# Adjacency blocks as sums of three bf16 products, with the one-hot operands of two blocks interleaved

## The reference, cut to what matters

```python
def _spmm(row, col, val, x):
    return jax.ops.segment_sum(val[:, None] * x[col], row, num_segments=N)
h = _spmm(edge_row, edge_col, edge_val, inputs_emb)
...
    z = _spmm(edge_row, edge_col, edge_val, outputs)      # layers 0 and 1
    AxW = jax.nn.softmax(z @ W.T + b, axis=1)
...
xn = _layernorm(x, axis=-1)
x = x + _L0_gnn_ref(xn, ..., edge_weight, src, dst) + _L0_mix_ref(xn[None], ...)[0]
x = x + _L0_ffn_ref(_layernorm(x, axis=-1)[None], ...)[0]
```

## Time and profile before

| | us |
|---|---|
| median of 3 runs | 1162.5 (1161.41 to 1164.13) |
| span of the profiled execution | 1161.9 |
| TensorE busy | 1097.3 (94%) |
| TensorE weight loads busy | 701.6 |
| VectorE busy | 737.1 (63%) |
| ScalarE busy | 314.2 (27%) |
| GpSimd busy | 168.1 (14%) |
| block matmuls (L1527), busy | 171.3 |
| products with the adjacency (L1542), busy | 291.8 |

### The profile page before, as it was taken

How to read it: one execution, slowest core, us unless ns; L and a number is a source line. 1 busy time by engine, 2 the same in 40 slices (tenths; PEclk the granted TensorE clock), 3 DMA queues, 4 the chain that set the end, 5 groups by cost and what they waited for, 6 DMA issues and landing times.

```text
span 1161.9 us, 14112 instructions
## 1 busy us (share of the span) xinstructions
PE 1097.3 (94%) x4837; PEld 701.6 (60%) x4837; DVE 737.1 (63%) x1681; ACT 314.2 (27%) x1038; POOL 168.1 (14%) x206
## 2 busy tenths in 40 slices
PE   5879999999999999999998999999998799999995
PEld 3446666666666666667793444644447666666664
DVE  8989989998786877777760111116788435554444
ACT  4667767421211222122210111101112211122220
POOL 1112223301010100000000000000234511111111
PEclk9899989999999999999998999999999799999998
DMA  5110111123323223343318998997995584555520
GB/s 168 18 45 13 46 47 46 46 91 121 133 96 133 114 112 121 126 154 136 131 57 323 325 354 292 343 343 275 308 320 213 155 217 117 118 141 136 141 63 7
DMA packets 78871, 178.52 MB, mean 154 GB/s; under 512 B 33567, under 2 KB 62011, under 8 KB 66639
## 3 DMA queue, kind: packets, MB, share of 16 engines
q1 hardware_dynamic: 67550, 126.16, 34.1%
q10 hardware_dynamic: 7120, 43.34, 9.2%
q0 software_dynamic: 4128, 8.08, 2.0%
HBM read 116.23 MB, written 63.77 MB: 155 GB/s over the span
## 4 chain that ended last, share of the span: by engine, by line
PE 80%; DVE 9%; SPq 3%; issue 3%; ACT 2%; DMA 1%; POOLq 0%; POOL 0%; ACTq 0%; DVEq 0%
PE ps L1542 21%; PE ps L1691 20%; PE ps L1527 11%; PE ps L1791 10%; PE ps L1779 9%; PE ps L1566 2%; SPq L465 2%; PE ps L1509 2%; PE ps L1442 1%; PE ps L1495 1%; DVE W L1022 1%; SPq L463 1%; DVE XT L1357 1%; ACT W L746 1%; PE ps L1516 1%
## 5 line engine op out<-in xcount | busy, mean ns | idle before, releaser
L1542 PE MATMUL ps<-RING,XX 128*128 128x512 f32 (+2 forms) x700 | 291.8, 542 | 1.0 <-DVE W L1082 1.0
L1691 PE MATMUL ps<-RING,RY 128*128 128x512 f32 (+4 forms) x750 | 273.7, 523 | 5.8 <-issue 5.8
L1691 PEld LDWEIGHTS ps<-RING,RY 128*128 128x128 f32 x750 | 136.8, 196 | 126.4 <-issue 119.0
L1527 PEld LDWEIGHTS ps<-RING 128*128 128x128 f32 x1250 | 164.5, 193 | 40.8 <-issue 34.1
L774 ACT COPY RING<-ps 128x512 f32<-128x512 f32 (+3 forms) x163 | 91.2, 560 | 312.2 <-PE ps L1527 298.2
L1527 PE MATMUL ps<-RING 128*128 128x128 f32 (+1 forms) x1250 | 171.3, 277 | 0.1
L1542 PEld LDWEIGHTS ps<-RING,XX 128*128 128x128 f32 x700 | 118.5, 191 | 68.8 <-issue 60.7
L1073 DVE TENSOR_TENSOR RING<-iota_n,RY 128x512 f32<-128x512 f32 (+1 forms) x138 | 91.2, 661 | 34.5 <-PE ps L1527 31.8
L1074 DVE TENSOR_TENSOR RING<-iota_n,RY 128x512 f32<-128x512 f32 (+1 forms) x138 | 100.5, 728 | 0.0
L1076 DVE TENSOR_TENSOR RING<-RING,RY 128x512 f32<-128x512 f32 (+1 forms) x138 | 91.1, 660 | 0.0
L900 ACT ACTIVATE RY<-ps,b1T 128x489 f32<-128x489 f32 x64 | 42.9, 670 | 172.2 <-PE ps L1779 172.2
(11 more groups left out here) (258 smaller groups left out, 1295.3 us busy)
## 6 DMA issues: line engine op xcount, KB each, us to landing
RING<-adj_dram SPq DMA_DIRECT2D x60, 1280.0 KB, 6.9
adj_dram<-RING ACTq DMA_DIRECT2D x30, 1280.0 KB, 4.5
rbuf_dram<-W SPq DMA_DIRECT2D x8, 516.0 KB, 5.4
RING<-rbuf_dram SPq DMA_DIRECT2D x8, 516.0 KB, 4.0
xbuf_dram<-W SPq DMA_DIRECT2D x8, 512.0 KB, 3.3
XT<-in_L_ffn_w SPq DMA_DIRECT2D x16, 256.0 KB, 5.1
XT<-in_L_ffn_w SPq DMA_DIRECT2D x4, 1024.0 KB, 8.4
RING<-in_L_ffn_w SPq DMA_DIRECT2D x16, 256.0 KB, 4.9
```

Source lines behind the costliest of these rows:

```text
L1527: last = nc.tensor.matmul(o[:, c:c + w], h[:, 0, i, :], h[:, 1, i, 0:w], start=True, stop=(j != s))
L1542: last = nc.tensor.matmul(ps[:, ACC + dd, 0:w], XN[:, j, dd * H:(dd + 1) * H], at[:, i * w:(i + 1) * w], start=(j == 0), stop=True, skip_g ...
L1691: last = nc.tensor.matmul(o, (Y if l == 0 else S0)[:, j, :], RING[:, slot_of[g % 5], i * across + first:i * across + first + w], start=(j ...
```

## The change

From unit 25 on a block is no longer one f32 product but the sum of three bf16 products: one one-hot matrix, all in bf16, times the other one-hot matrix multiplied by each of the three bf16 pieces of the value. The value now goes into the second operand. The operands of two neighbouring blocks are interleaved, so that the last dimension of every operand of VectorE is a pair of bf16 numbers (`pair_b`), and TensorE reads every second element. `recs` becomes a bf16 table; the f32 sum of the pieces, which only the lead needs, goes into `lead_w`. So that pairs begin at even groups, the extra group of the diagonal blocks is moved from place 25 to place 23 (`SPARE`), and tiles 23 and 24 to places 24 and 25 (`place_in`). Strip 5 works on two pairs, the second with the extra group as its unused half. A diagonal block takes three more products from `own_src` and `own_val`, which VectorE makes in four small operations. In the lead the matmuls stay in f32; ScalarE scales the extra group too, in four units.

```diff
+SPARE = 23
...
+def place_in(t):
+    return t if t < SPARE else t + 1
...
-        recs = RY[:, 0:5 * NG].rearrange("p (f n) -> p f n", f=5)
+        recs = RY[:, 0:1625].bitcast(BF16).rearrange("p (f n) -> p f n", f=5)
+        lead_w = RY[:, 1626:2276]
...
-        hot = [ring[:, 7680 + 1280 * i:8960 + 1280 * i].rearrange("p (a g n) -> p a g n", a=2, n=P) for i in range(4)]
+        hot_w = [ring[:, 7680 + 1280 * i:8960 + 1280 * i] for i in range(4)]
+        hot = [h.rearrange("p (a g n) -> p a g n", a=2, n=P) for h in hot_w]
+        hot_b = [h.bitcast(BF16) for h in hot_w]
+        pair_b = [h[:, 0:2048].rearrange("p (a c k i) -> p a c k i", a=4, c=2, i=2) for h in hot_b]
+        own_src = [h[:, 2048:2176] for h in hot_b]
+        own_val = [h[:, 2176:2560].rearrange("p (a k) -> p a k", a=3) for h in hot_b]
...
+        iota_p = sb("iota_p", [P, 2 * P], BF16)
...
-            gp.iota(ints[:, 416:416 + SW], pattern=[[1, NR], [0, WC]], base=0, channel_multiplier=0).then_inc(s_const, 1)
+            gp.iota(ints[:, 416:416 + SPARE * WC], pattern=[[1, SPARE], [0, WC]], base=0, channel_multiplier=0).then_inc(s_const, 1)
+            gp.iota(ints[:, 416 + SPARE * WC:416 + (SPARE + 1) * WC], pattern=[[0, WC]], base=EXTRA, channel_multiplier=0).then_inc(s_const, 1)
+            gp.iota(ints[:, 416 + (SPARE + 1) * WC:416 + SW], pattern=[[1, NT - SPARE], [0, WC]], base=SPARE, channel_multiplier=0).then_inc(s_const, 1)
...
+                    whole = lead_w[:, j * NR:(j + 1) * NR]
                     gp.wait_ge(s_recrd, j + 1)
-                    gp.tensor_tensor(w1, w1, w2, ALU.add).then_inc(s_wpart, 1)
+                    gp.tensor_tensor(whole, w1, w2, ALU.add).then_inc(s_wpart, 1)
                     gp.wait_ge(s_wpart, j + 1)
-                    gp.tensor_tensor(w1, w1, w3, ALU.add).then_inc(s_wsum, 1)
+                    gp.tensor_tensor(whole, whole, w3, ALU.add).then_inc(s_wsum, 1)
...
-                for i, (j, s) in enumerate(UNITS[u]):
-                    last = nc.scalar.activation(hot[u % 4][:, 0, i, :], hot[u % 4][:, 0, i, :], ACT.Copy, scale=recs[:, 2, j * NR + s:j * NR + s + 1])
+                blocks = list(enumerate(UNITS[u])) + [(4, (j, SPARE)) for j, s in UNITS[u] if j == s]
+                for i, (j, s) in blocks:
+                    last = nc.scalar.activation(hot[u % 4][:, 0, i, :], hot[u % 4][:, 0, i, :], ACT.Copy, scale=lead_w[:, j * NR + s:j * NR + s + 1])
...
+            v.tensor_scalar(iota_p[:, :], ints[:, 160:160 + 2 * P], -1.0 - OWN, None, ALU.add)
...
-                h = hot[u % 4]
+                own = [t for t, g in b if t == g]
                 if u < LEAD:
                     dve.wait_ge(s_wsum, u + 1)
-                own = [t for t, g in b if t == g]
-                if own:
-                    i = own[0] * NR + EXTRA
-                    v.tensor_scalar(h[:, 0, 4, :], iota_n[:, :], recs[:, 0, i:i + 1], recs[:, 2, i:i + 1], ALU.is_equal, ALU.mult)
-                    v.tensor_scalar(h[:, 1, 4, :], iota_n[:, :], recs[:, 1, i:i + 1], None, ALU.is_equal)
-                if u < LEAD:
+                    h = hot[u % 4]
+                    for t in own:
+                        i = t * NR + SPARE
+                        for a in range(2):
+                            v.tensor_scalar(h[:, a, 4, :], iota_n[:, :], recs[:, a, i:i + 1], None, ALU.is_equal)
                     v.tensor_tensor(h[:, :, 0:n, :], iota_n[:, :].unsqueeze(1).unsqueeze(1).to_broadcast([P, 2, n, P]),
                                     recs[:, 0:2, j * NR + s:j * NR + s + n].unsqueeze(3).to_broadcast([P, 2, n, P]), ALU.is_equal).then_inc(s_hot, 1)
                     return
-                if u < NT * (NS - 1):
-                    grid = lambda f: recs[:, f, j * NR + s:j * NR + s + n].unsqueeze(2).to_broadcast([P, n, P])
-                    every = iota_n[:, :].unsqueeze(1).to_broadcast([P, n, P])
-                    block = lambda a: h[:, a, 0:n, :]
-                else:
-                    grid = lambda f: recs[:, f, :].rearrange("p (t g) -> p t g", g=NR)[:, j:j + n // 2, s:s + 2].unsqueeze(3).to_broadcast([P, n // 2, 2, P])
-                    every = iota_n[:, :].unsqueeze(1).unsqueeze(1).to_broadcast([P, n // 2, 2, P])
-                    block = lambda a: h[:, a, 0:n, :].rearrange("p (t g) n -> p t g n", g=2)
-                v.tensor_tensor(block(0), every, grid(0), ALU.is_equal).then_inc(s_eq, 1)
-                v.tensor_tensor(block(1), every, grid(1), ALU.is_equal)
+                if u == LEAD:
+                    dve.wait_ge(s_recrd, NT)
+                heads = [j * NR + s, j * NR + s + 2] if u < NT * (NS - 1) else [t * NR + place_in(s) for t in range(j, j + n // 2)]
+                views = [(pair_b[u % 4][:, :, c], recs[:, :, first:first + 2], iota_p[:, :].rearrange("p (k i) -> p k i", i=2)) for c, first in enumerate(heads)]
+                for h, fields, every in views:
+                    wide = lambda x, m: x.unsqueeze(2).to_broadcast([P, m, P, x.shape[-1]])
+                    last = v.tensor_tensor(h[:, 0:4:3], every.unsqueeze(1).to_broadcast([P, 2, P, fields.shape[-1]]), wide(fields[:, 0:2], 2), ALU.is_equal)
+                last.then_inc(s_eq, 1)
+                for t in own:
+                    i = t * NR + SPARE
+                    v.tensor_scalar(own_src[u % 4], iota_n[:, :], recs[:, 0, i:i + 1], None, ALU.is_equal)
+                    for f in range(3):
+                        v.tensor_scalar(own_val[u % 4][:, f, :], iota_n[:, :], recs[:, 1, i:i + 1], recs[:, 2 + f, i:i + 1], ALU.is_equal, ALU.mult)
                 dve.wait_ge(s_eq, u + 1 - LEAD)
-                v.tensor_tensor(block(0), block(0), grid(2), ALU.mult).then_inc(s_hot, 1)
+                for h, fields, every in views:
+                    last = v.tensor_tensor(h[:, 1:4], h[:, 3:4].to_broadcast([P, 3, P, fields.shape[-1]]), wide(fields[:, 2:5], 3), ALU.mult)
+                last.then_inc(s_hot, 1)
...
+                piece = lambda a, i, w: pair_b[u % 4][:, a, i // 2, 0:w, i % 2]
                 ge(pe, s_bev, u - 1)
                 pe.wait_ge(s_wgt if u < LEAD else s_hot, u + 1)
                 for i, (j, s) in enumerate(UNITS[u]):
-                    c = width(g for _, g in UNITS[u][:i])
+                    c = width(t for _, t in UNITS[u][:i])
                     w = width([s])
-                    last = nc.tensor.matmul(o[:, c:c + w], h[:, 0, i, :], h[:, 1, i, 0:w], start=True, stop=(j != s))
+                    if u < LEAD:
+                        last = nc.tensor.matmul(o[:, c:c + w], h[:, 0, i, :], h[:, 1, i, 0:w], start=True, stop=(j != s))
+                        if j == s:
+                            last = nc.tensor.matmul(o[:, c:c + w], h[:, 0, 4, :], h[:, 1, 4, 0:w], start=False, stop=True)
+                        continue
+                    for f in range(3):
+                        last = nc.tensor.matmul(o[:, c:c + w], piece(0, i, P), piece(1 + f, i, w), start=(f == 0), stop=(f == 2 and j != s))
                     if j == s:
-                        last = nc.tensor.matmul(o[:, c:c + w], h[:, 0, 4, :], h[:, 1, 4, 0:w], start=False, stop=True)
+                        for f in range(3):
+                            last = nc.tensor.matmul(o[:, c:c + w], own_src[u % 4], own_val[u % 4][:, f, 0:w], start=False, stop=(f == 2))
```

More of the change, by code:

```diff
@@ L619, in _ @@
                              base=0, pattern=[[1, P]], channel_multiplier=-1).then_inc(s_const, 1)
-            gp.wait_ge(s_const, 9)
+            gp.wait_ge(s_const, 11)
             gp.memset(blk, 0.0).then_inc(s_blk, 1)
@@ L705, in _ @@
             act.dma_start(wv_n, half("L0_mix_wv")).then_inc(s_kvw, 16)
-            act.wait_ge(s_const, 9)
+            act.wait_ge(s_const, 11)
             nc.scalar.copy(before[:, :], before_f).then_inc(s_constb, 1)
@@ L941, in _ @@
             v.tensor_scalar(tile_no[:, :], thr[:, :], 1.0 / P, None, ALU.mult)
-            dve.wait_ge(s_const, 6)
+            dve.wait_ge(s_const, 8)
             v.tensor_copy(iota_n[:, :], ints[:, 32:32 + P])
             v.tensor_copy(iota_k[:, :], ints[:, 160:160 + 2 * P])
+            v.tensor_scalar(iota_p[:, :], ints[:, 160:160 + 2 * P], -1.0 - OWN, None, ALU.add)
             dve.wait_ge(s_dst, 16)
@@ L953, in _ @@
             v.tensor_scalar(base_i[:, :], base_f, 0.0, float(E - WIN), ALU.max, ALU.min).then_inc(s_base, 1)
-            dve.wait_ge(s_const, 9)
+            dve.wait_ge(s_const, 11)
             dve.wait_ge(s_blk, 3)
@@ L1442, in flip @@
                 return nc.tensor.transpose(dst, src, ident[0:n, 0:n])
-            pe.wait_ge(s_const, 9)
+            pe.wait_ge(s_const, 11)
             pe.wait_ge(s_cnt0, 1)
```

## The result

The changed kernel takes 1143.4 us (median of 4 runs, 1141.83 to 1146.42) against 1162.5 us before on the same chip: a ratio of 0.9837, 95% interval 0.982 to 0.9853. That is 19.1 us less, as forecast.

A forecast was written before the change was run, and what follows sets the result against it. The prediction took TensorE, busy 94% of 1161.9 us, to bound the kernel. 20.5 us from the blocks less 1.4 of waits gave 19.1, so 1162.5 - 19.1 = 1143.4 us, range 1134 to 1152.

The forecast's parts named there:

- What bounds: Strips 1 to 5: TensorE has no margin, so a microsecond saved there is the kernel's, as long as VectorE follows.
- TensorE per block: Block build from unit 25: three bf16 matmuls at 0.061 us replace 0.2225 us; 0.0395 us gained, times 520 is 20.5 us.
- that same form: The lead's bf16 slot matmuls, 130 columns picked from pairs, 0.061 us apart, taken as the spacing of the new block matmuls.
- case E: Block matmuls come near the streaming rate, 0.055 us each: 1133.5 us at the end of it; chance 12%.
- Narrow blocks: Last strip's 26 blocks of 53 columns: no gain counted, since no row showed so narrow a bf16 matmul.
- VectorE per unit: Operand building: 1.73 us a unit, 0.08 less than now; 2.59 against 2.26 with a diagonal block.
- case B: VectorE takes one element at a time: 3.05 us a unit, kernel slower at 1221 us; chance 3%.
- Waits that take some back: TensorE waiting for VectorE in strip 1 and the last strip gives back 1.4 us of the gain.
- the three places named: TensorE waits: key-value product in strip 1, 1.0 us; copy at strip 1's start, 0.1 lost; last strip's copy, 0.3 lost.
- What costs nothing: Start and lead: an added constant, two GpSimd iotas and ScalarE scalings in units 0 to 3 hide in idle time.
- The stage behind: After the last build and a 5.77 us gap, the next stage starts as now and moves as a whole.
- D: No change in time: what is saved is waited for behind the stage; chance 3%.

The follow-up runs named there:

- One product of three: Changed kernel keeping only the first of a block's three bf16 products, the diagonal's extra product cut likewise: 1104.7 us for 1171.8 before, 0.9428.
- the pairs: Changed kernel with two units built in a row, then two applied, from unit 26 on: 0.9900 of the kernel before.
- the unpaired layout: Changed kernel with the two blocks of a pair side by side, not interleaved: 1268.7 us for 1171.8 before, 1.0827.
- `both`: Changed kernel with units built and applied two at a time from unit 26, plus later key-value products and spread hidden-node steps: 0.9876 of before.

## Why the prediction held, step by step

- **What bounds.** Right. One product of three moves the kernel by what TensorE saves, 0.058 us a matmul from unit 50 to unit 124.
- **TensorE per block.** The mechanism was right (more and shorter passes, less time), the size too small: 0.0395 us forecast, 0.050 measured, and 520 x 0.0105 = 5.5 us more gain. The failed choice was to take the slot matmuls' 61 ns for "that same form". The streaming rate in the same group, 0.055 (case E), was nearer to the measured 0.0575.
- **The f32 products behind the build.** This term was missing. 0.05 us in 125 units and 0.02 in 13: 6.5 us lost. One product of three and the pairs both show that it goes by the number of changes from bf16 to f32, not by the number of matmuls. Why is not settled. The f32 load has a mean of 191 ns in the trace, and behind a 57 ns matmul less of it is covered than behind a 111 ns pass:

```profile
L1571 PEld LDWEIGHTS ps<-RING,XX 128*128 128x128 f32 x700 | 118.1, 191 | 69.9 <-issue 62.1
```

  That fits. So does the last strip, where a narrow matmul stands ahead of the f32 group in both kernels: the group's first pass takes 0.219 us before and 0.236 after, its later ones 0.153 in both. But no run took it apart.
- **Narrow blocks.** Nothing forecast; 0.22 us a unit, 13 units: 2.9 us gained.
- **VectorE per unit.** 1.73 and 2.59 forecast, 1.74 and 2.58 measured. The row of L1022 was the right one, and the unpaired layout gave the price of case B, 3.06 for 3.05.
- **Waits that take some back.** 1.4 us forecast; the three places named measure 0.87 + 0.10 + 0.33 = 1.3. That moving the first one wins nothing shows that it was rightly put down to VectorE's work in strip 1. The 0.3 of the last strip was luck: it took over 0.5 us for what TensorE's three units save, where two full-width blocks a unit at 0.0395 us make 0.24. And the five waits at the strips' starts, 0.96 us, were missing, against the forecast's "nowhere else in strips 1 to 4": the copy that it reckoned with at the start of strip 1 stands ahead of every strip. With them it is 2.3 us.
- **What costs nothing.** Right: 0.9993 with the lead's edits alone.
- **The stage behind.** Right: D is out. The gap in the chain is 5.66 us for 5.77, and what follows its start is 1.7 us shorter than before, not longer. The same gap in the chain of the kernel with one product, and then of `both`, whose spans are 1103.1 and 1154.7 us:

```profile
549.73 5.83 issue
```

```profile
600.89 5.87 issue
```

From there to the end it is 553.4 and 553.8 us, though the one starts 51 us before the other: the stage behind moves along as a whole.

The new sum is 26.0 - 6.5 + 2.9 - 2.3 = 20.1 us for the stage, and 20.3 are measured. By stretch the same terms give 2.9 for strip 1 (2.8 measured), 11.3 for strips 2 to 4 (11.7), 2.5 for strip 5 (2.8) and 3.3 for the last strip (3.0), each within 0.4 us. The forecast of 19.1 was close by luck in its terms: 5.5 too little for the blocks and 2.9 for the narrow ones stood against 6.5 for the f32 passes and 0.9 for the waits that it didn't have. By stretch the 2.3 us that the last strip gave beyond the forecast (3.0 against 0.7) more than make up for the 1.0 that the others fell short.

The rule that spoke against the change, the Trainium skill's 81 ns per matmul at 128 columns in a stream of loads and matmuls ("TensorE: Matmul & The Clock Gate", Back-to-back issue gap), doesn't hold here: 57.4 ns in such a stream. The gap that the same section gives for a single matmul, N / 2.4 + 2.5 or 56 ns, is close to what these kernels show, about 56 with neighbouring elements and 57.4 with every second one.

## What to carry to other kernels

Where TensorE is full, an f32 product with a one-hot operand can be had as three bf16 products at 0.172 us instead of 0.222 per 128 x 128 block, if the cutting into pieces is already done and the engine that makes the operands can follow; count the change of type between groups too, 0.05 us each here, a quarter of what a unit gained. Lay bf16 operands out so that the last dimension of every VectorE operand is a pair of real neighbours, even if TensorE must then read at a stride: that cost TensorE under 2 ns a matmul and took VectorE from 3.06 to 1.74 us a unit. Before moving a consumer away from a wait, look whether its producer is late with everything; if so the wait only moves on. And where a producer's copy stands at the seam between two stretches, a shorter operation ahead of its consumer gains nothing: here 0.2 us at each strip's start.

## What the runs showed of the hardware

- bf16 matmuls of 128 columns, each with its load of 128, start 57.4 ns apart, whether the stationary operand is the one before or another, and in groups of 4, 12 and 24 alike. The loads are recorded at a mean of 97 ns:

```profile
L1555 PEld LDWEIGHTS ps<-RING 128*128 128x128 bf16 x1575 | 100.6, 97 | 50.0 <-issue 43.3
```

- One f32 matmul of 128 columns (0.2225 us, two records) takes as long as four of the bf16 ones with neighbouring elements (about 0.056 us each), which is why three of them for one pay.
- With 53 columns and the same load they start about 27 ns apart: the load of 128 columns sets no floor at 57 ns.
- The first f32 pass of 512 columns behind a bf16 group takes 0.48 us to the next start instead of 0.43, with 4, 12 or 24 bf16 matmuls ahead of it.
- VectorE's bf16 operations in pairs cost 0.95 us for 2 x 768 elements, and 1.74 where one operand repeats a single number in its last dimension.
